# Moving the product of block one-hots and token numbers from VectorE to GpSimd

## The reference

```python
def _L0_ffn_ref(x, Wg, W1, b1, W2, b2):
    logits = jnp.einsum('btc,ce->bte', x, Wg)
    probs = jax.nn.softmax(logits, axis=-1)
    top_vals, top_idx = jax.lax.top_k(probs, 2)
    gates = (jax.nn.one_hot(top_idx, E) * top_vals[..., None]).sum(-2)
    h = jax.nn.relu(jnp.einsum('btc,ech->bteh', x, W1) + b1)
    y = jnp.einsum('bteh,ehc->btec', h, W2) + b2
    return jnp.einsum('bte,btec->btc', gates, y)
h = _layernorm(h + _L0_ffn_ref(h, ...), axis=-1)
```

## Time and profile before

| what | value |
|---|---|
| median of 3 runs | 333.32 us (330.98, 333.32, 427.85) |
| the profiled execution | 333.53 us, of which the span of the profile is 331.7 us |
| TensorE busy | 297.0 us, 90% of the span |
| VectorE busy | 159.9 us, 48% |
| GpSimd busy | 119.7 us, 36% |
| ScalarE busy | 105.5 us, 32% |
| mean granted TensorE clock | 0.943 of full |

### The profile page before, as it was taken

The page is one execution under the profiler, slowest core; times in us unless marked ns, Lnnn a source line. Parts: engine busy times, 40 slices in busy tenths (PEclk is TensorE's granted clock), DMA queues, the critical chain, the costliest instruction groups (busy, mean ns, idle before and its releaser), DMA issues.

```text
span 331.7 us, 6654 instructions
## 1 busy us (share of the span) xinstructions
PE 297.0 (90%) x2638; PEld 248.5 (75%) x2638; DVE 159.9 (48%) x471; ACT 105.5 (32%) x252; POOL 119.7 (36%) x182
## 2 busy tenths in 40 slices
PE   8969689998699999999999987987888979999991
PEld 8946478975499899999999944875565765758780
DVE  4878553559311221011101029468789636384765
ACT  5768327141011111111110200657423120583230
POOL 8761200283604383343342222651653200063312
PEclk9999855787899999999999999999999999999997
DMA  7999200010118678999997050000000000000002
GB/s 264 375 326 324 67 0 0 26 50 2 48 25 305 210 256 264 299 293 282 311 287 244 14 148 25 2 0 3 2 4 0 2 2 0 0 4 2 2 2 74
DMA packets 12033, 37.68 MB, mean 114 GB/s; under 512 B 1914, under 2 KB 5882, under 8 KB 11771
## 3 DMA queue, kind: packets, MB, share of 16 engines
q1 hardware_dynamic: 10083, 33.32, 30.8%
q0 software_dynamic: 1920, 3.93, 4.0%
HBM read 34.06 MB, written 3.19 MB: 112 GB/s over the span
## 4 chain that ended last, share of the span: by engine, by line
PE 69%; DVE 15%; issue 5%; DMA 4%; POOL 3%; ACT 3%; SPq 0%; POOLq 0%; DVEq 0%
PE ps L893 11%; PE ps L880 8%; PE ps L881 8%; PE ps L923 4%; PE ps L958 4%; PE ps L644 3%; PE ps L1072 3%; DMA xs<-x_rows,from_row 2%; PE ps L755 2%; PE ps L771 2%; PE ps L934 2%; PE ps L944 2%; PE ps L969 1%; PE ps L671 1%; DVE st L1731 1%
## 5 line engine op out<-in xcount | busy, mean ns | idle before, releaser
L880 PE MATMUL ps<-xga,w1t 128*128 128x128 f32 x240 | 47.4, 279 | 0.0
L881 PE MATMUL ps<-xgb,w1u 65*128 65x128 f32 x240 | 47.4, 279 | 0.0
L1263 ACT ACTIVATE hid<-ps 128x768 f32<-128x768 f32 x20 | 16.2, 810 | 93.4 <-PE ps L881 93.4
L1680 DVE COPY ys<-ps 128x192 f32<-128x192 f32 x20 | 7.1, 357 | 79.8 <-PE ps L893 75.7
L893 PE MATMUL ps<-w1t,hid 128*128 128x192 f32 x240 | 42.2, 326 | 0.0
L558 POOL DMA_INDIRECT y_rows<-ys,to_row x20 | 19.8, 988 | 59.5 <-DVE ys L1680 59.2
L893 PEld LDWEIGHTS ps<-w1t,hid 128*128 128x128 f32 x240 | 38.6, 190 | 0.0
L880 PEld LDWEIGHTS ps<-xga,w1t 128*128 128x128 f32 x240 | 37.3, 195 | 0.0
L881 PEld LDWEIGHTS ps<-xgb,w1u 65*128 65x128 f32 x240 | 37.3, 195 | 0.0
L644 PE MATMUL ps<-w1a,consts 128*128 128x384 f32 x92 | 35.5, 518 | 1.3 <-DVE h_tok L1552 1.3
L597 POOL COPY v_bd<-v_f 32x192 f32<-32x192 f32 x64 | 22.5, 351 | 35.6 <-ACT v_f L1142 31.8
(11 more groups left out here) (257 smaller groups left out, 585.0 us busy)
## 6 DMA issues: line engine op xcount, KB each, us to landing
w1t<-in_wt SPq DMA_DIRECT2D x20, 960.0 KB
w1u<-in_wu SPq DMA_DIRECT2D x20, 240.0 KB
pat<-in_pat SPq DMA_DIRECT2D x6, 496.0 KB, 5.8
w1a<-in_w1a SPq DMA_DIRECT2D x1, 1322.0 KB
y<-y_rows SPq DMA_DIRECT2D x6, 192.0 KB, 3.2
w1b<-in_w1b SPq DMA_DIRECT2D x1, 835.2 KB
x_rows<-x_tok SPq DMA_DIRECT2D x3, 192.0 KB, 2.0
out<-x_tok SPq DMA_DIRECT2D x6, 96.0 KB, 1.7
```

The lines of the kernel that those rows point to most:

```text
L880: pe.matmul(out, w1t[:, b, 128 * k:128 * k + 128], xga[:, j % 2, :], start=True, stop=False)
L881: mm = pe.matmul(out, w1u[0:CB + 1, b, 128 * k:128 * k + 128], xgb[:, j % 2, :], start=False, stop=True)
L1263: act.activation(hid[:, j % 2, :], z, ACT.Relu).then_inc(hid_done, 1)
```

## The change

GpSimd makes blk_ids in place of VectorE. VectorE's in_blk no longer waits for its own end (its `link` goes) but raises a new semaphore, blk_hot; VectorE goes on to the two halves of in_row at once. GpSimd, ahead of its waits for the gathers, waits for blk_hot, makes the same product with the same operands, raises blk_ids_ready and waits for that itself. TensorE waits for blk_ids_ready, besides the first half of in_row, before the first of the 14 matmuls. Nothing else is changed.

```diff
@@ gpsimd, ahead of the first gathers
+            pool.wait_ge(blk_hot, 1)
+            one = in_blk[:, :, :]
+            pool.tensor_tensor(blk_ids[:, :, :, :], bass.AP(tensor=one.tensor, offset=one.offset, ap=[list(d) for d in one.ap] + [[0, 3]]),
+                               view(ids, [[3, PICKS], [0, NBLK], [1, 3]]), ALU.mult).then_inc(blk_ids_ready, 1)
+            pool.wait_ge(blk_ids_ready, 1)
             pool.wait_ge(rows_out, 16 * PAIRS)
             pool.wait_ge(from_ready, 1)
@@ tensor
             for i in range(PICKS):
                 if i % TT == 0:
                     pe.wait_ge(onehot_ready, i // TT + 1)
+                    if i == 0:
+                        pe.wait_ge(blk_ids_ready, 1)
@@ vector
-            link(dve.tensor_tensor(in_blk[:, :, :], over(slots[:, 1, :], NBLK), view(iota_blk, [[0, PICKS], [1, NBLK]]), ALU.is_equal))
-            dve.tensor_tensor(blk_ids[:, :, :, :], over(in_blk[:, :, :], 3), view(ids, [[3, PICKS], [0, NBLK], [1, 3]]), ALU.mult)
+            dve.tensor_tensor(in_blk[:, :, :], over(slots[:, 1, :], NBLK), view(iota_blk, [[0, PICKS], [1, NBLK]]), ALU.is_equal).then_inc(blk_hot, 1)
             for k in range(TOPK):
                 part = slice(TT * k, TT * k + TT)
                 dve.tensor_tensor(in_row[:, part, :], over(slot_row[:, part], 128), view(iota128, [[0, TT], [1, 128]]), ALU.is_equal).then_inc(onehot_ready, 1)
```

More of the change, by code:

```diff
@@ L279, in build @@
         onehot_ready, ids_ready = sem("onehot_ready"), sem("ids_ready")
+        blk_hot, blk_ids_ready = sem("blk_hot"), sem("blk_ids_ready")
         from_ready, to_ready, expert_ready = sem("from_ready"), sem("to_ready"), sem("expert_ready")
```

## The result

The changed kernel took 338.65 us in the median of six runs (336.83 to 340.26), the kernel before 334.35 in the median of six (five of them 330.98 to 337.75, the sixth 427.85, which nothing here explains). The ratio is 1.0158, with a 95% interval of 1.0092 to 1.0223: in these runs slower by about 4 us, where +0.74 was forecast. The profiled execution took 338.96 us with a span of 337.0, at a mean granted clock of 0.927 against 0.943.

A forecast was written before the change was run, and what follows sets the result against it. TensorE, busy nine tenths of the span, was taken as the bound, with the routing chain setting when the experts start. A 1.03 us product leaves VectorE, a 1.8 us wait replaces it: +0.74, forecast 334.1 us, range 331.0 to 335.9.

The forecast's parts named there:

- The port and its turns: Routing: GpSimd's product and VectorE's in_row halves exclude each other at the SBUF port, running first half, product, second half.
- The size of the product: GpSimd's blk_ids product, at the f32 subtraction's 2.17 ns an element: 1.99 us for 840 elements, 1.84 us behind the port.
- the sum: Routing: first half ends 80.29, product 82.13, second half 83.10; `found` starts at 83.65 in place of 82.91, +0.74 us.
- (a): Routing: the engines don't exclude each other, or GpSimd is fast as a fill; gain capped at 0.35 us; chance 0.13.
- (b): Routing: turns go otherwise or GpSimd is slower; +0.85 to +1.97 us, 334.2 to 335.3 from the median; chance 0.18.
- The cap by the dummies: Routing: TensorE's dummies delay its first seven matmuls to 81.63 whatever VectorE does, so the gain is at most about 0.35 us.
- (c): First expert block: TensorE's low-clock stretch grows through added gaps; slower by more than 2%, 340 us or more; chance 0.02.
- (d): First expert block: TensorE's low-clock stretch falls away, 1.7 us less, giving 332.4 us; chance 0.04.

The follow-up runs named there:

- e5: The changed kernel run again with no edit, third group of runs: 336.59 us, ratio 1.0003 to the kernel before.
- e6: The changed kernel with iota128 copied by ScalarE to PSUM, where in_row reads it: 332.94 us, ratio 0.9958 to the kernel before.
- e9: Null: the kernel before, unedited, in the place of the changed one: 336.72 us, ratio 1.0076.
- e14: The changed kernel run again with no edit, on one chip with a null: 336.10 us, ratio 1.0003 to the kernel before.
- e8: The changed kernel run again with no edit, beside a null: 338.27 us in six runs, too few for a ratio.
- e1: The changed kernel run again with no edit, first repeat: 334.91 us, ratio 0.9966 to the kernel before.
- e7: The changed kernel with iota128 in PSUM for in_row and four dummies in place of five ahead of the 14 matmuls: 332.76 us, ratio 0.9939 to the kernel before.
- e10: The kernel with iota128 in PSUM, with the inputs of GpSimd's product in f32 in place of bf16: product 1.67 us against 1.61, no device time given.
- e16: The version with iota128 in PSUM and four dummies, once more on another chip: 333.47 us, ratio 0.9956 to the kernel before.
- e2: The kernel before with two more linked 0.20 us steps on VectorE ahead of in_blk: 335.35 us, ratio 0.9973.
- e11: The kernel before with one linked 0.20 us step on VectorE between the experts and the late attention: 335.30 us, ratio 0.9993.
- e12: The kernel before with four linked 0.20 us steps on VectorE between the experts and the late attention: 335.57 us, ratio 1.0040.

## Why the prediction was wrong

**The port and its turns: right.** The first half of in_row unharmed, then the product, then the second half, each whole, in every profile of the changed kernel; with PSUM in place of one SBUF input the waiting goes. The rule of the Trainium skill (SBUF — State Buffer, section "SBUF: two separate sides") holds here: 2501 ns for the half that met the product, 1082 where in_row had one SBUF input.

**The size of the product: mis-sized.** The term of 1.84 us behind the port measured 1.47 us. I had taken the subtraction's 2.17 ns an element; it was 1.75 (1.47 us for 840). That takes 0.37 of the 0.74 off. The second half behind it took 0.96 us; the sum's 0.43 + 0.56 makes 0.99, and the 0.97 written there was a slip that did no harm. The routing's price is +0.34, between the ends of (a) and (b) and of the right sign.

**The cap by the dummies: wrong.** "The most that the edit can gain on this path is about 0.35 us" rested on dummies that end near 81.7. They took 4.26 us in that execution, where TensorE's clock was 0.50 until 79.1 us, and 3.49 in e5 and e6, at 1.00. e6 gained 0.84. In e5, the changed kernel, the first seven matmuls wait for the product, as the edit would have it:

```profile
75.86 3.49 PE L650 MATMUL ps<-w1a,consts 128*128 128x384 f32 x10
80.87 0.46 PE L866 MATMUL ps<-blk_ids,in_row 128*128 128x60 bf16 x7 [1.51 <-POOL blk_ids L563]
```

I had read a length that depends on the clock as a fixed one. The forecast of +0.74 doesn't use the cap; the price of rival (a) does.

**The clock: the step that failed.** The range's end, 335.9, was built as the upper bound of (b) on one profiled execution "with some room for the clock". Rival (c) looked for the clock only at the first expert block, the one low stretch that the rows of before showed near the change, and (d) priced its absence. The price of (c) was mis-stated besides: 6 us more of expert work at the low level are 12 us on top of the 3.6, not in their place. The trace of before had no fall in the late attention, so no term stood for it, and the sum took every stretch behind the routing to shift at its length. What failed is this: the clock behind the experts stood at nothing, without a reason, where the changed kernel took 29.58 us in place of 25.13. Yet that stretch had the gaps. The same instructions, in TensorE's timeline of the kernel before,

```profile
236.85 0.85 PE L934 MATMUL ps<-k_bd,qT 64*32 64x100 f32 x48 [1.05 <-ACT qT L1142]
238.23 0.55 PE L944 MATMUL ps<-consts,p 128*128 128x128 f32 x3 [0.54 <-POOL p L607]
238.71 1.17 PE L958 MATMUL ps<-p1T,v_bd 128*64 128x25 f32 x24
239.80 0.91 PE L644 MATMUL ps<-w1a,consts 128*128 128x384 f32 x2
240.65 0.85 PE L934 MATMUL ps<-k_bd,qT 64*32 64x100 f32 x48
```

and of the changed one:

```profile
237.68 0.85 PE L942 MATMUL ps<-k_bd,qT 64*32 64x100 f32 x48 [1.05 <-ACT qT L1150]
239.07 0.55 PE L952 MATMUL ps<-consts,p 128*128 128x128 f32 x3 [0.54 <-POOL p L613]
239.55 1.44 PE L966 MATMUL ps<-p1T,v_bd 128*64 128x25 f32 x24
240.91 1.65 PE L650 MATMUL ps<-w1a,consts 128*128 128x384 f32 x2
242.49 1.25 PE L942 MATMUL ps<-k_bd,qT 64*32 64x100 f32 x48
```

Ahead of the fall TensorE waited 1.05 and 0.54 us in both, had the same work in between, and ran it at full clock in the one; in the other the low level came at 240.3, and the dummies took 1.65 us in place of 0.91. What a trace of one execution shows at full clock, another execution of the same kernel can show at the low level: the null e9 has a fall at 239.8 us in its profile, and runs of the kernel before reach 342 and more. I took the nearness of a few runs (2.5 us) for the scatter; 165 runs of it reach from 330.96 to 351.88 us and have 38 above 336.8.

**What stays open.** Whether the change also makes the late falls more frequent. 23 of 48 runs of the changed kernel lie above 336.8 us, 17 of 42 without the first six, against 38 of 165 of the kernel before; each repeat but e14 has the higher share. Chance would part 17 of 42 from 38 of 165 so far, in this direction, about one time in fifty, if runs are independent, and the null e9 makes that doubtful; 23 of 48 is just under the half that I had set as the mark with e14. All five profiles of the changed kernel have TensorE at the low level somewhere from 236 to 265 us (three falls in the first, e5 and e8, one in e14, one of 10.3 us in e1), and one of the three of the kernel before has it (e9). Of the four kernels with iota128 in PSUM three show it (some 24 us in e6 and e7, three falls in e10), though the runs of e6, e7 and e16 lie above 336.8 us in only 6 of 39. A shift in the routing (e2, 3 of 12) or behind it (e11, 2 of 12) doesn't bring the share up; the larger shift of e12 (5 of 12) may. The ratios of e1, e5 and e14, 0.9966, 1.0003 and 1.0003, leave no difference to explain in what is compared there. The 4.3 us of the first result are not the change's reproducible price, and why the clock was low in all six of those runs isn't known.

## What to carry to other kernels

Before handing GpSimd a product to run "beside" VectorE, look at what VectorE runs meanwhile: with two inputs in SBUF the two took turns here, and the chain got the sum; with one input moved to PSUM they overlapped. A change worth 0.3 us in a kernel whose time the clock spreads over 20 us is read from the stretch in the trace (4.09, 4.43, 3.25), the same within 0.01 us in every profile, and not from the device time. And one trace at full clock says nothing of the next execution: a stretch where TensorE waits a microsecond at a time, as it does in this late attention, is a risk to put into the range, though that the waits bring the falls is argued here and not shown.

## What the runs showed that I had not expected

GpSimd's product of 840 elements with repeated reads ran at 1.9 ns an element free of the port (1.61 us in e6 and e7), start-up included, against 2.4 for the f32 subtraction of 768. And the falls of TensorE's clock in executions of one and the same kernel spread its time from 331 to 352 us, nearly along one line of 0.26 us for each 0.001 of mean granted clock (the 427.85 us of an early run aside).
